# Two graph attention layers on one core: the second MLP product in 512 and 256 columns, with two sums added on VectorE, and new orders for all engines

## The chip, the core and the metric

One core of a Trainium2 chip runs the whole program. The metric is the device time of one execution in microseconds. Before the change it was 2083.72 us, the median of 3 runs (2083.6 to 2084.96).

## What is computed

x is 128 graphs x 128 nodes x 256 features in float32, adj a 128x128 matrix of 0 and 1 for each graph. Layer 0 is masked attention with 8 heads of 32, a residual and a normalisation. Layer 1 normalises, attends with a mask that also carries 0.1 x adj as a bias, adds the residual, normalises again and adds an MLP. Cut to what matters here:

```python
    x1 = residual + (out @ wo + bo)
    n2 = _ln(x1, ln2_g, ln2_b)
    mlp = jax.nn.gelu(n2 @ w1 + b1, approximate=False) @ w2 + b2      # w1 256x1024, w2 1024x256
    return x1 + mlp
```

## The kernel before, in words

**Tiling.** The 128 graphs are worked on in 32 groups b of G = 4 graphs; a group has T = 512 rows. A product whose operands carry real precision is split: each operand is a high part (float32r) and a low part, the remainder, and three products high x high, high x low and low x high are summed in PSUM (`split_mm`, lines 497 to 502, its matmuls at line 500). For q, k and the first MLP product (`qkv` n = 0 to 3, `mlp_up`) the moving operand has 512 columns; for v, the output projection and the second MLP product (`qkv` n = 4, 5, `out_proj`, `mlp_down`) it has 256.

**mlp_down(b, g)**, lines 557 to 567, takes graph g of a group: 8 chunks of 128 of the 1024 hidden features, three products each, the stationary operand being a chunk of h (high, high, low) and the moving one the 256 columns of w2 (high, low, high). Two graphs fill one PSUM bank ("MLP2", j), which VectorE adds to x1 in one operation of 128x512, `residual("MLP2", b, j)` (lines 972 to 981, the addition at 980).

**Attention.** `scores` (line 470) issues 32 small matmuls for half a group on 32-row tiles of the array. VectorE adds the mask and takes the maximum (`mask_scores`, 919), ScalarE takes the exponential (`exp`, 687), VectorE the reciprocal of the sum (`recip`, 935), GpSimd scales (`normalise`, 1147), TensorE transposes (`flip`, 482), ScalarE and VectorE copy the result into pt (`copy_pt`, 697 and 942), and `values` (493) multiplies by v, again in halves of 32 small matmuls. `flip_rows` (511) transposes the normalised rows for the next layer.

**Order.** Each engine has an order written out by hand: a head for groups 0 to 4, a body repeated for i = 5 to 30, which mixes stages of groups i + 1 to i - 3, and a tail. PSUM's 8 banks are handed out by the table JOBS (name, number, how many groups behind, bank); `open_job` makes TensorE wait until the bank's last user is done, `filled` makes a reader wait for TensorE, and `taken` waits for the reader. In the body before, the two halves of values of a group stand apart, with flips, products or transposes between them.

**Once, at the start.** The load of x for group 0 (transposed, xTr) is the first in ScalarE's DMA queue (line 660), ahead of the small table of columns (661). SyncE's queue starts with wq, wk, wv of layer 0 (384), then the two copies of adj. VectorE splits wq, wk and wv and then subtracts the high part of x (`x_lo`, 962). `second_products` (lines 445 to 456) makes 36 matmuls, 32 of them of one column at line 454, to fold constant shifts into biases; it needs w1 and stands behind the first out_proj of group 0's second half. `store` writes x1 out when the last MLP2 addition is done.

Of the kernel before, what the change touches and what calls it, by code (L numbers as in the profile page):

```python
# [160 lines left out]

def program(nc, x, xT, adj, w):
    ctx = ExitStack()
    with ctx:
# [1116 lines left out]
```

## Time and profile before

| what | us |
|---|---|
| median of 3 runs | 2083.72 |
| the profiled execution | 2083.27 |
| its span | 2081.5 |
| TensorE (PE) busy | 2039.3 |
| TensorE weight loads (PEld) busy | 1829.3 |
| ScalarE (ACT) busy | 1651.2 |
| VectorE (DVE) busy | 1596.7 |
| GpSimd (POOL) busy | 1008.5 |

The mean granted TensorE clock is 0.993 of full. Busy means that at least one instruction of the engine was in work. Matmuls overlap, so a record's duration (283 ns for 256 columns) is not what one adds: the distance from one start to the next is. The profiled execution's own time is 1.8 us more than its span, and 0.45 us less than the median.

### The profile page before, as it was taken

How to read it: one execution, taken by the hardware profiler on the slowest of the kernel's cores; microseconds unless marked ns; L12 is line 12 of the kernel's file. 1: busy time of each engine (PE TensorE's matmuls, PEld its weight loads, DVE VectorE, ACT ScalarE, POOL GpSimd, SP SyncE). 2: the span in 40 equal slices, each digit the busy share in tenths (PEclk: the TensorE clock that was granted, in tenths of full speed). 3: DMA queues.
4: the chain of work that ended last, by engine and by line, in shares of the span. 5: the costliest groups of instructions: out<-in, count | busy, mean ns of one | idle time of the engine just before them, and what ended most of it. 6: DMA issues, size and time to landing. Idle time of an engine off the chain costs nothing.

```text
span 2081.5 us, 58805 instructions
## 1 busy us (share of the span) xinstructions
PE 2039.3 (98%) x20032; PEld 1829.3 (88%) x20032; DVE 1596.7 (77%) x6915; ACT 1651.2 (79%) x5512; POOL 1008.5 (48%) x780
## 2 busy tenths in 40 slices
PE   6899999999999999999999999999999999999997
PEld 5688998889989889998889988889988899998886
DVE  6887877787877787777787777778777878777763
ACT  4788887888787878788888888887878887878873
POOL 3645445545445545445545445445455455455431
PEclk9999999999999999999999999999999999999999
DMA  5011110111110111100111100111101111101000
GB/s 155 17 32 42 43 38 15 30 41 41 40 34 14 33 40 41 41 19 21 40 41 41 40 10 30 41 40 41 38 13 30 41 41 40 35 15 31 27 12 21
DMA packets 80830, 73.18 MB, mean 35 GB/s; under 512 B 3024, under 2 KB 72272, under 8 KB 80720
## 3 DMA queue, kind: packets, MB, share of 16 engines
q1 hardware_dynamic: 80304, 71.45, 10.9%
q8 instruction: 36, 0.59, 0.1%
q14 instruction: 74, 0.61, 0.1%
q10 hardware_dynamic: 416, 0.54, 0.1%
HBM read 55.20 MB, written 16.78 MB: 35 GB/s over the span
## 4 chain that ended last, share of the span: by engine, by line
PE 96%; DVE 2%; ACT 1%; issue 0%; DMA 0%; POOL 0%; ACTq 0%; SPq 0%; DVEq 0%
PE ps L500 68%; PE ps L482 11%; PE ps L470 7%; PE ps L493 6%; PE ps L511 3%; ACT pm L687 1%; DVE pm L919 1%; DMA pm<-in_wk 0%; DVE stats L993 0%; PE ps L454 0%; DVE pt L942 0%; ACT k L721 0%; POOL pm L1147 0%; POOL rstd L1166 0%; DVE bv_rows L837 0%
## 5 line engine op out<-in xcount | busy, mean ns | idle before, releaser
L1147 POOL TENSOR_TENSOR pm<-pm,rinv 128x512 f32<-128x512 f32 x512 | 521.8, 1042 | 602.9 <-DVE rinv L935 602.7
L687 ACT ACTIVATE pm<-pm,nmax 128x128 f32<-128x128 f32 x2048 | 792.2, 392 | 10.1 <-DVE nmax L919 9.5
L919 DVE CUSTOM_DVE_ANT_0 pm<-ps,m 128x128 f32<-128x128 f32 x2048 | 456.4, 285 | 43.6 <-PE ps L470 42.5
L687 ACT ACTIVATION_READ_ACCUMULATOR pm<-pm,nmax 128x1 f32 x2048 | 392.3, 192 | 0.0
L500 PE MATMUL ps<-w2h,hh 128*128 128x256 f32 x1024 | 294.7, 288 | 2.2 <-DVE hl L1015 2.1
L482 PE MATMUL ps<-ident,pm 128*128 128x128 f32 x2048 | 289.7, 277 | 2.9 <-DVE v L968 1.8
L500 PE MATMUL ps<-w2h,hl 128*128 128x256 f32 x1024 | 289.6, 283 | 0.0
L500 PE MATMUL ps<-w2l,hh 128*128 128x256 f32 x1024 | 289.6, 283 | 0.0
L1166 POOL TENSOR_TENSOR rstd<-veps,power 128x4 f32<-128x4 f32 x96 | 97.3, 1014 | 362.4 <-DVE veps L1001 362.0
L482 PEld LDWEIGHTS ps<-ident,pm 128*128 128x128 f32 x2048 | 230.6, 140 | 45.6 <-issue 18.3
L942 DVE COPY pt<-ps 128x512 f32<-128x512 f32 x256 | 175.5, 687 | 104.7 <-PE ps L482 104.6
L697 ACT ACTIVATE pt<-ps 128x512 f32<-128x512 f32 x256 | 151.0, 591 | 105.8 <-PE ps L482 105.8
L1015 DVE TENSOR_TENSOR hl<-ps,hh 128x512 fp32r<-128x512 f32 x256 | 169.9, 681 | 61.5 <-ACT ps L745 58.0
L500 PE MATMUL ps<-acth,w1h 128*128 128x512 f32 x512 | 210.2, 410 | 3.8 <-DVE actl L956 3.8
L500 PE MATMUL ps<-acth,w1l 128*128 128x512 f32 x512 | 201.7, 394 | 0.0
L500 PE MATMUL ps<-actl,w1h 128*128 128x512 f32 x512 | 201.1, 393 | 0.0
L500 PEld LDWEIGHTS ps<-w2h,hh 128*128 128x128 f32 x1024 | 196.1, 192 | 4.2 <-DVE hl L1015 3.0
L500 PEld LDWEIGHTS ps<-w2l,hh 128*128 128x128 f32 x1024 | 196.3, 192 | 1.2
L500 PEld LDWEIGHTS ps<-w2h,hl 128*128 128x128 f32 x1024 | 196.1, 191 | 0.0
L744 ACT ACTIVATE hh<-ps,b 128x512 fp32r<-128x512 f32 x256 | 180.0, 703 | 14.1 <-PE ps L500 11.8
L745 ACT ACTIVATE ps<-ps,b 128x512 f32<-128x512 f32 x256 | 173.4, 677 | 0.0
L919 DVE DVE_READ_ACCUMULATOR2_ANT nmax<- 128x1 f32 x2048 | 170.2, 83 | 0.0
(123 smaller groups left out, 5058.7 us busy)
## 6 DMA issues: line engine op xcount, KB each, us to landing
xy<-in_x SPq DMA_DIRECT2D x32, 512.0 KB, 5.3
xTr<-in_xT SPq DMA_DIRECT2D x31, 512.0 KB, 4.5
out<-x SPq DMA_DIRECT2D x31, 512.0 KB, 3.0
m<-in_adj SPq DMA_DIRECT2D x32, 256.0 KB, 2.8
a<-in_adj SPq DMA_DIRECT2D x32, 256.0 KB, 2.8
pt<-in_w SPq DMA_DIRECT2D x2, 512.0 KB, 8.5
pt<-in_w SPq DMA_DIRECT2D x1, 1024.0 KB, 11.6
xTr<-in_xT ACTq DMA_DIRECT2D x1, 512.0 KB, 5.1
```

The lines of the kernel that those rows point to most:

```text
L470: last = mm(outs[r][:, at:at + N], q[l][rows, c, gs], k[l][rows, c, gs], start=True, stop=True)
L482: last = nc.tensor.transpose(out[:, j * N:(j + 1) * N], pm[:, g, c * HC + j, :], ident[:, :])
L493: last = mm(out[j * HD:(j + 1) * HD, at:at + N], v[l][:, g, h * HD:(h + 1) * HD], pt[:, pt_slot(l, g), place(h), :], start=True, stop=True)
L500: last = mm(out, pick(parts[a], c), wpick(wparts[b], c), start=(n == 0), stop=(n == len(terms) - 1))
L687: last = nc.scalar.activation(pm[:, g, h, :], pm[:, g, h, :], ACT.Exp, bias=nmax[:, g, h:h + 1], scale=-1.0, accum_out=rsum[:, g, h:h + 1])
L697: nc.scalar.activation(pt[:, pt_slot(l, g), 0:HC, :], src[:, :].rearrange("p (h q) -> p h q", h=HC), ACT.Copy).then_inc(free_of(f"F{l}", 2 ...
L744: nc.scalar.activation(hh[0][:, m, :], src[:, :], ACT.Gelu, bias=b1[:, m:m + 1])
L745: nc.scalar.activation(src[:, :], src[:, :], ACT.Gelu, bias=b1[:, m:m + 1]).then_inc(h_hi, 1)
L919: last = nc.vector.tensor_tensor_reduce(out=pm[:, g, h, :], in0=src[:, at:at + N], in1=m[:, g, :], scale=1.0, scalar=3e38, op0=ALU.add, op ...
L942: nc.vector.tensor_copy(pt[:, pt_slot(l, g), HC:H, :], src[:, :].rearrange("p (h q) -> p h q", h=HC))\
L1015: tt(hh[1][:, m, :], bank_of("MLP1", m)[:, :], hh[0][:, m, :].bitcast(F32), ALU.subtract).then_inc(free_of("MLP1", m), 1)
L1147: tt(pm[:, g, hs, :], pm[:, g, hs, :], rinv[:, g, hs].rearrange("p (h a) -> p h a", a=1).to_broadcast([P, HC, N]), ALU.mult).then_inc(norm ...
```

## The change

- mlp_down: for each chunk one product of 512 columns, the high part of h against both parts of w2, which now lie side by side in w2_both, and one of 256 columns, the low part of h against the high part of w2, summed into the right half of the bank. Each graph has a bank of its own. Two sums come out: left high x high, right the two cross terms.
- VectorE adds both to x1, one after the other, in operations of 128x256 (`residual_down`).
- The two halves of values of a layer stand next to each other in TensorE's order.
- The load of x for group 0 is second in SyncE's queue, behind wq. VectorE subtracts x's high part before it splits wk and wv, and wv is split only after mask0.
- second_products comes before the third flip of group 0.
- JOBS, HEAD, TAIL (the banks) and the orders of TensorE, ScalarE, VectorE and GpSimd are written anew.

```diff
-        w2 = [sb(f"w2{p}", [P, FC, D], F32R) for p in "hl"]
+        w2_both = sb("w2", [P, FC, 2, D], F32R)
+        w2 = [w2_both[:, :, p, :] for p in (0, 1)]
...
-                        taken(sp, b, "MLP2", j)
+                        taken(sp, b, "MLP2", 2 * j + 1)
...
-                    taken(sp, b, "MLP2", 1)
+                    taken(sp, b, "MLP2", G - 1)
...
+                    if n == 0:
+                        sp.dma_start(xTr[:, :, :], xT_v[:, :, 0:T]).then_inc(xT_loaded, 16)
...
+            def paired_mm(out, parts, pick, both, chunks):
+                for c in range(chunks):
+                    if c:
+                        mm(out[:, D:], pick(parts[1], c), both(c)[:, 0, :], start=False, stop=False)
+                    last = mm(out[:, :], pick(parts[0], c), both(c), start=(c == 0), stop=(c == chunks - 1))
+                    if c == 0:
+                        mm(out[:, D:], pick(parts[1], c), both(c)[:, 0, :], start=False, stop=False)
+                return last
...
-                    out = open_job(b, "MLP2", g // 2) if g % 2 == 0 else bank_of("MLP2", g // 2)
-                    last = split_mm(out[:, (g % 2) * D:(g % 2 + 1) * D], hh, w2,
-                                    lambda t, c: t[:, c, g * N:(g + 1) * N], lambda t, c: t[:, c, :], FC)
-                    if g % 2 == 1:
-                        full(last, "MLP2", g // 2)
+                    out = open_job(b, "MLP2", g)
+                    last = paired_mm(out, hh, lambda t, c: t[:, c, g * N:(g + 1) * N], lambda c: w2_both[:, c, :, :], FC)
+                    full(last, "MLP2", g)
...
-                sc.dma_start(xTr[:, :, :], xT_v[:, :, 0:T]).then_inc(xT_loaded, 16)
                 sc.dma_start(par[:, :], w["columns"]).then_inc(cols_loaded, 16)
...
+                        if l == 0 and first(b):
+                            dve.wait_ge(wqkv_lo[0], 3 * C)
...
+            def residual_down(b, g):
+                if exists(b):
+                    dve.wait_ge(x1b_done, b + 1)
+                    src = filled(dve, b, "MLP2", g)
+                    tt(x1[:, g, :], src[:, :D], x1[:, g, :], ALU.add).then_inc(half_sum, 1)
+                    dve.wait_ge(half_sum, slot(b, g) + 1)
+                    tt(x1[:, g, :], src[:, D:], x1[:, g, :], ALU.add).then_inc(free_of("MLP2", g), 1)
```

TensorE's body after, in full (that before is in the listing above):

```python
            def body(i):
                flip_rows("T2", i - 3, 1); scores(Y, i - 2, 0); flip(X, i - 1, 1, 1); flip(X, i - 1, 2, 0)
                mlp_up(i - 3, 0); mlp_up(i - 3, 1); flip(X, i - 1, 2, 1); mlp_up(i - 3, 2); flip(X, i - 1, 3, 0)
                mlp_up(i - 3, 3); flip(X, i - 1, 3, 1); mlp_up(i - 3, 4); values(X, i - 1, 0); values(X, i - 1, 1)
                mlp_up(i - 3, 5); mlp_up(i - 3, 6); mlp_up(i - 3, 7); out_proj(X, i - 1, 0); out_proj(X, i - 1, 1)
                scores(Y, i - 2, 1); flip(Y, i - 2, 0, 0); qkv(X, i, 0); qkv(X, i, 1); qkv(X, i, 2); qkv(X, i, 3)
                mlp_down(i - 3, 0); mlp_down(i - 3, 1); flip(Y, i - 2, 0, 1); scores(X, i, 0); flip(Y, i - 2, 1, 0)
                flip(Y, i - 2, 1, 1); mlp_down(i - 3, 2); mlp_down(i - 3, 3); flip(Y, i - 2, 2, 0); qkv(X, i, 4)
                flip(Y, i - 2, 2, 1); flip(Y, i - 2, 3, 0); flip(Y, i - 2, 3, 1); qkv(X, i, 5)
                flip_rows("T1", i - 1, 0); values(Y, i - 2, 0); values(Y, i - 2, 1); scores(X, i, 1)
                flip_rows("T1", i - 1, 1); flip(X, i, 0, 0); out_proj(Y, i - 2, 0); out_proj(Y, i - 2, 1)
                flip(X, i, 0, 1); flip(X, i, 1, 0); qkv(Y, i - 1, 0); qkv(Y, i - 1, 1); qkv(Y, i - 1, 2)
                qkv(Y, i - 1, 3); qkv(Y, i - 1, 4); qkv(Y, i - 1, 5); flip_rows("T2", i - 2, 0)
```

The part of VectorE's body around the new additions:

```python
                residual("WO0", i - 1, 1); mask_scores(Y, i - 2, 2, 0); mask_scores(Y, i - 2, 2, 1)
                mask_scores(Y, i - 2, 3, 0); mask0(i); recip(Y, i - 2, 1); norm_stats(0, i - 1)
                mask_scores(Y, i - 2, 3, 1); norm_rows(0, i - 1); residual_down(i - 3, 0); residual_down(i - 3, 1)
                recip(Y, i - 2, 2); copy_pt(Y, i - 2, 0); mask_scores(X, i, 0, 0); mask_scores(X, i, 0, 1)
                recip(Y, i - 2, 3); flipped(Y, i - 2, 1, 0); mask_scores(X, i, 1, 0); flipped(Y, i - 2, 1, 1)
                mask_scores(X, i, 1, 1); residual_down(i - 3, 2); norm_stats(1, i - 1); copy_pt(Y, i - 2, 1)
                residual_down(i - 3, 3); norm_rows(1, i - 1); copy_pt(Y, i - 2, 2); copy_pt(Y, i - 2, 3)
```

The new JOBS gives MLP2's four products the banks 6, 4, 6 and 7; flip (1, 1) of layer 1 has bank 4, and the scores of X, half 0, have banks 7, 0, 3 and 1.

## Rows read from the trace of the kernel before

**Rows 1.** The page: busy us and count of two engines; the chain by engine.
```profile
PE 2039.3 (98%) x20032; PEld 1829.3 (88%) x20032; DVE 1596.7 (77%) x6915; ACT 1651.2 (79%) x5512; POOL 1008.5 (48%) x780
...
PE 96%; DVE 2%; ACT 1%; issue 0%; DMA 0%; POOL 0%; ACTq 0%; SPq 0%; DVEq 0%
```

**Rows 2.** TensorE's waits: who waited for whom, us in total, times, longest.
```profile
PE ps L493 <- DVE pt L942: 3.8, 1, 3.8
```

**Rows 3.** Busy us (and count) of PE, PEld, DVE, ACT, POOL by stretch; clock; DMA.
```profile
968.60:1031.60 63.00, 63.00 (x625) 56.63 (x625) 49.24 (x215) 51.39 (x173) 31.27 (x25) 1.00 0.11 34
...
276.00:1913.00 1637.00, 1637.00 (x16224) 1471.95 (x16223) 1279.93 (x5591) 1335.50 (x4473) 812.35 (x625) 1.00 0.11 34
```

**Rows 4.** TensorE's timeline, 1028 to 1040 us: start, duration, instruction.
```profile
1029.10 0.39 PE L500 MATMUL ps<-actl,wqkv0h 128*128 128x512 f32 x1
...
1032.98 0.28 PE L500 MATMUL ps<-w2h,hh 128*128 128x256 f32 x1
1033.09 0.28 PE L500 MATMUL ps<-w2l,hh 128*128 128x256 f32 x1
...
1038.73 0.40 PE L500 MATMUL ps<-acth,wqkv0h 128*128 128x512 f32 x1
...
1039.20 0.39 PE L500 MATMUL ps<-acth,wqkv0l 128*128 128x512 f32 x1
```

**Rows 5.** Weight loads by line and form: busy us, mean ns, idle before.
```profile
L500 PEld LDWEIGHTS ps<-w2h,hl 128*128 128x128 f32 x1024 | 196.1, 191 | 0.0
```

**Rows 6.** TensorE's timeline, 1043 to 1047 us.
```profile
1043.96 1.17 PE L470 MATMUL ps<-k,q 32*128 32x128 f32 x32
...
1046.07 1.09 PE L482 MATMUL ps<-ident,pm 128*128 128x128 f32 x8
1046.92 0.36 PE L500 MATMUL ps<-w2h,hh 128*128 128x256 f32 x1
```

**Rows 7.** The weight loads' timeline in the same stretch.
```profile
1045.06 0.81 PEld L493 LDWEIGHTS ps<-pt,v 128*32 128x32 f32 x32
1046.07 0.86 PEld L482 LDWEIGHTS ps<-ident,pm 128*128 128x128 f32 x8 [0.20 <-issue]
```

**Rows 8.** VectorE by line and form: busy us, mean ns, idle before.
```profile
L980 DVE TENSOR_TENSOR x<-ps,x 128x512 f32<-128x512 f32 x64 | 42.6, 665 | 12.9 <-PE ps L500 12.9
...
L998 DVE BATCH_NORM_AGGREGATE mv<-stats 128x2 f32<-128x6 f32 x384 | 36.8, 157 | 14.4 <-issue 0.4
...
L873 DVE TENSOR_TENSOR bo<-bo,ps 128x256 f32<-128x256 f32 x1 | 0.4, 408 | 0.0
```

**Rows 9.** The timeline of all engines, 0 to 12 us.
```profile
0.74 0.51 ACTq L660 DMA_DIRECT2D xTr<-in_xT  x1
...
6.73 0.49 DVE L825 TENSOR_SCALAR wqkv0h<-pm 128x256 fp32r<-128x256 f32 x2
6.92 0.20 ACT L656 ACTIVATE nbq<-par 128x2 f32<-128x2 f32 x1 [3.85 <-DMA par<-in_columns]
7.16 1.15 ACT L737 ACTIVATE acth<-xTr 128x512 fp32r<-128x512 f32 x2
...
9.60 1.29 DVE L962 TENSOR_TENSOR actl<-xTr,acth 128x512 fp32r<-128x512 f32 x2
...
11.04 0.77 PE L500 MATMUL ps<-acth,wqkv0h 128*128 128x512 f32 x1 [11.04 <-DVE actl L962]
```

**Rows 10.** The chain that ended last, in order of time.
```profile
45.96 4.43 PE ps L454 x32
```

**Rows 11.** DMA issues: KB each, median us from issue to landing.
```profile
pt<-in_w SPq DMA_DIRECT2D x2, 512.0 KB, 8.5
...
xTr<-in_xT ACTq DMA_DIRECT2D x1, 512.0 KB, 5.1
```

**Rows 12.** The timeline of all engines, 2078 us to the end.
```profile
2077.83 0.28 PE L500 MATMUL ps<-w2h,hl 128*128 128x256 f32 x1
2078.21 0.69 DVE L980 TENSOR_TENSOR x<-ps,x 128x512 f32<-128x512 f32 x1 [5.07 <-PE ps L500]
```

More of the change, by code:

```diff
@@ L642, in tail @@
                 mlp_down(30, 1); mlp_down(30, 2); flip(Y, 31, 1, 0); flip(Y, 31, 1, 1); mlp_down(30, 3)
-                flip(Y, 31, 2, 0); flip(Y, 31, 2, 1); flip(Y, 31, 3, 0); flip(Y, 31, 3, 1); values(Y, 31, 0)
-                values(Y, 31, 1); out_proj(Y, 31, 0); out_proj(Y, 31, 1); flip_rows("T2", 31, 0)
+                flip(Y, 31, 2, 0); flip(Y, 31, 2, 1); flip(Y, 31, 3, 0); flip(Y, 31, 3, 1)
+                values(Y, 31, 0); values(Y, 31, 1); out_proj(Y, 31, 0); out_proj(Y, 31, 1); flip_rows("T2", 31, 0)
@@ L847, in split_q, with split_kv, first_rows @@
                 split_part(0, -SCALE)
[L849 removed]
+            def split_kv(b, n):
                 if first(b):
[L851 to L852 removed]
+                    split_part(n, 1.0)
+            def first_rows(b):
+                if first(b):
                     dve.wait_ge(cols_loaded, 16)
@@ L1060, in head @@
-                split_h(1, 4); out_lo(X, 3, 1); split_h(1, 5); mask0(4); split_h(1, 6); x_lo(4, 0); x_lo(4, 1)
-                residual("WO0", 3, 1); split_h(1, 7); norm_stats(0, 3); mask_scores(Y, 2, 2, 0); recip(Y, 2, 1)
-                norm_rows(0, 3); mask_scores(Y, 2, 2, 1); copy_pt(Y, 2, 0); mask_scores(Y, 2, 3, 0)
-                residual("MLP2", 1, 0); copy_pt(Y, 2, 1); recip(Y, 2, 2); mask_scores(Y, 2, 3, 1); norm_stats(1, 3)
-                recip(Y, 2, 3); mask_scores(X, 4, 0, 0); mask_scores(X, 4, 0, 1); mask_scores(X, 4, 1, 0)
@@ L1065, in head @@
-                mask_scores(X, 4, 1, 1); out_lo(Y, 2, 0); norm_rows(1, 3); v_out(X, 4, 0); recip(X, 4, 0)
-                residual("MLP2", 1, 1); v_out(X, 4, 1); copy_pt(Y, 2, 2); copy_pt(Y, 2, 3); lo("T1", 3, 0)
-                lo("T1", 3, 1); mask1(3); out_lo(Y, 2, 1); mask_scores(X, 4, 2, 0); residual("WO1", 2, 0)
-                mask_scores(X, 4, 2, 1); recip(X, 4, 1); residual("WO1", 2, 1); mask_scores(X, 4, 3, 0)
-                norm_stats(2, 2); mask_scores(X, 4, 3, 1); copy_pt(X, 4, 0); norm_rows(2, 2); v_out(Y, 3, 0)
@@ new lines, in head @@
+                copy_pt(X, 0, 1); copy_pt(X, 0, 2); split_qkv1(0, 1); copy_pt(X, 0, 3); out_lo(X, 0, 0); x_lo(1, 0)
+                x_lo(1, 1); out_lo(X, 0, 1); residual("WO0", 0, 0); mask0(1); residual("WO0", 0, 1); norm_stats(0, 0)
+                norm_rows(0, 0); mask_scores(X, 1, 0, 0); mask_scores(X, 1, 0, 1); mask_scores(X, 1, 1, 0)
+                mask_scores(X, 1, 1, 1); norm_stats(1, 0); v_out(X, 1, 0); v_out(X, 1, 1); recip(X, 1, 0)
+                norm_rows(1, 0); mask_scores(X, 1, 2, 0); lo("T1", 0, 0); lo("T1", 0, 1); recip(X, 1, 1)
@@ new lines, in head @@
+                mask_scores(X, 1, 2, 1); mask_scores(X, 1, 3, 0); copy_pt(X, 1, 0); split_w1(0, 0); recip(X, 1, 2)
+                mask_scores(X, 1, 3, 1); split_w1(0, 1); v_out(Y, 0, 0); mask_scores(Y, 0, 0, 0); recip(X, 1, 3)
+                mask_scores(Y, 0, 0, 1); mask_scores(Y, 0, 1, 0); flipped(X, 1, 1, 1); mask_scores(Y, 0, 1, 1)
+                copy_pt(X, 1, 1); copy_pt(X, 1, 2); copy_pt(X, 1, 3); v_out(Y, 0, 1); out_lo(X, 1, 0); recip(Y, 0, 0)
+                x_lo(2, 0); mask0(2); residual("WO0", 1, 0); recip(Y, 0, 1); x_lo(2, 1); mask_scores(Y, 0, 2, 0)
@@ new lines, in head @@
+                out_lo(Y, 0, 0); lo("T1", 1, 0); out_lo(Y, 0, 1); mask_scores(X, 2, 2, 0); mask_scores(X, 2, 2, 1)
+                lo("T1", 1, 1); recip(X, 2, 1); residual("WO1", 0, 0); residual("WO1", 0, 1); mask_scores(X, 2, 3, 0)
+                norm_stats(2, 0); copy_pt(X, 2, 0); mask_scores(X, 2, 3, 1); norm_rows(2, 0); mask1(1); recip(X, 2, 2)
+                v_out(Y, 1, 0); lo("T2", 0, 0); lo("T2", 0, 1); mask_scores(Y, 1, 0, 0); mask_scores(Y, 1, 0, 1)
+                mask_scores(Y, 1, 1, 0); copy_pt(X, 2, 1); mask0(3); recip(X, 2, 3); copy_pt(X, 2, 2); v_out(Y, 1, 1)
@@ new lines, in head @@
+                flipped(X, 2, 1, 1); mask_scores(Y, 1, 1, 1); copy_pt(X, 2, 3); split_h(0, 0); split_h(0, 1)
+                out_lo(X, 2, 0); split_h(0, 2); split_h(0, 3); split_h(0, 4); split_h(0, 5); out_lo(X, 2, 1)
+                x_lo(3, 0); x_lo(3, 1); residual("WO0", 2, 0); recip(Y, 1, 0); split_h(0, 6); residual("WO0", 2, 1)
+                split_h(0, 7); norm_stats(0, 2); mask_scores(Y, 1, 2, 0); mask_scores(Y, 1, 2, 1); recip(Y, 1, 1)
+                mask_scores(Y, 1, 3, 0); mask_scores(Y, 1, 3, 1); norm_rows(0, 2); residual_down(0, 0)
@@ new lines, in head @@
+                lo("T1", 2, 1); mask_scores(X, 3, 2, 1); residual("WO1", 1, 0); residual("WO1", 1, 1); recip(X, 3, 1)
+                mask_scores(X, 3, 3, 0); norm_stats(2, 1); mask_scores(X, 3, 3, 1); copy_pt(X, 3, 0); norm_rows(2, 1)
+                mask1(2); recip(X, 3, 2); v_out(Y, 2, 0); lo("T2", 1, 0); lo("T2", 1, 1); mask_scores(Y, 2, 0, 0)
+                mask_scores(Y, 2, 0, 1); recip(X, 3, 3); mask_scores(Y, 2, 1, 0); copy_pt(X, 3, 1)
+                flipped(X, 3, 1, 1); mask_scores(Y, 2, 1, 1); recip(Y, 2, 0); copy_pt(X, 3, 2); copy_pt(X, 3, 3)
@@ new lines, in head @@
+                split_h(1, 0); v_out(Y, 2, 1); split_h(1, 1); out_lo(X, 3, 0); split_h(1, 2); out_lo(X, 3, 1)
+                split_h(1, 3); mask0(4); split_h(1, 4); split_h(1, 5); x_lo(4, 0); residual("WO0", 3, 0)
+                split_h(1, 6); x_lo(4, 1); split_h(1, 7); residual("WO0", 3, 1); mask_scores(Y, 2, 2, 0)
+                norm_stats(0, 3); mask_scores(Y, 2, 2, 1); mask_scores(Y, 2, 3, 0); mask_scores(Y, 2, 3, 1)
+                recip(Y, 2, 1); norm_rows(0, 3); residual_down(1, 0); copy_pt(Y, 2, 0); residual_down(1, 1)
@@ new lines, in head @@
+                residual("WO1", 2, 0); residual("WO1", 2, 1); mask_scores(X, 4, 3, 0); norm_stats(2, 2)
+                mask_scores(X, 4, 3, 1); copy_pt(X, 4, 0); norm_rows(2, 2); mask1(3); recip(X, 4, 2); v_out(Y, 3, 0)
+                lo("T2", 2, 0); lo("T2", 2, 1); mask_scores(Y, 3, 0, 0); recip(X, 4, 3); mask_scores(Y, 3, 0, 1)
+                mask_scores(Y, 3, 1, 0); flipped(X, 4, 1, 1); mask_scores(Y, 3, 1, 1); copy_pt(X, 4, 1)
+                copy_pt(X, 4, 2); recip(Y, 3, 0); v_out(Y, 3, 1); copy_pt(X, 4, 3); split_h(2, 0); split_h(2, 1)
```

484 lines of the change are left out of this document (221 added, 263 removed), and 137 rows, old and new, of tables (HEAD, JOBS, TAIL).

## The prediction, made before the changed kernel ran

> **What bounds the kernel now.** I began with the page's busy times and chain [rows 1]: TensorE is busy for 2039.3 of 2081.5 us and 96% of the chain that ended last is its matmuls; VectorE has a quarter of the span free. As a busy share proves little for pipelined matmuls, I next asked for TensorE's waits [rows 2]. They are few, and all of them lie in the first 110 us or the last 110: the same question for 276 to 1913 us returned no line. The table of stretches [rows 3] says so in another way: in one loop of 62.97 us (968.6 to 1031.6, repeated 26 times) TensorE has no idle time, VectorE is busy for 49.24 us, ScalarE for 51.39 and the clock is granted in full. So in the loop only a shorter stream of TensorE instructions saves time, and work put on another engine is free until it makes TensorE wait.
>
> The profiled execution took 2083.27 us, 1.8 beyond its span; the median of the runs is 2083.72, 0.45 more. I work from 2083.27. About 0.2% (4 us) is what a measurement of this kernel can tell from no change.
>
> **The paired product.** For each of 8 chunks of h and 4 batch rows, mlp_down issued three products of 256 columns; now there is one of 512 (high h against both parts of w2) and one of 256 (low h): 1024 chunks in 32 groups, 2048 matmuls in place of 3072, over the same 768 columns. The timeline [rows 4] gives the pace from start to start: 48 matmuls of 256 columns take 5.75 us (1032.98 to 1038.73), 119.8 ns each; 17 of 512 columns take 3.88 us (1029.10 to 1032.98), 228 ns each. Two of 256 cost 240 ns, one of 512 costs 228. A chunk goes from 359.4 to 228 + 119.8 = 348 ns: 11.4 ns x 1024 = **11.7 us saved**. No row shows the two lengths alternating, as they will now, so I bound a pair by the changeovers: the first two of 512 after a run of 256 took 0.47 us, 235 ns each (pair 355 ns, 4.5 us saved), and the first of 256 after one of 512 took 0.11 (pair near 339, 21 us saved). I take the middle, since it is what each has in its own run, and keep both ends.
>
> Every matmul comes with a weight load of its own, which lasts 192 ns in the records [rows 5] and yet is issued every 119.8, so loads overlap matmuls here. The Trainium skill ("TensorE: Matmul & The Clock Gate", Back-to-back issue gap) gives 262 cycles for 256 columns and 518 for 512, so by it three become one and one for 6 cycles, an estimated 2.5 ns a chunk and 2.6 us in all, which speaks against most of this gain. What the rows would make of such a rule is the first rival below.
>
> **A layer's values as one step.** values ran as two halves of 32 small matmuls with other work between; now both halves of a layer stand together. One half takes 1.01 us (1045.06 to 1046.07) and scores 1.10 [rows 6, 7]. The weight path stood idle for 0.20 us behind the half before it could turn to flips [rows 7]. Inside a half one group of 4 follows another every 0.09 to 0.11 us (32 in 0.81 us of loads), so a half that follows a half should save 0.20 - 0.09 = 0.11 us. In the loop the counts are equal otherwise: scores and values form five runs per loop before and five after, and two borders between scores and values become two between halves. 62 pairs x 0.11 = **6.8 us saved** (nothing if the border stays, 12 if all 0.20 goes).
>
> **The other order of TensorE.** By the two written orders, the loop has 13 runs of flips and transposes in place of 12. Their own work is the same; 8 flips behind values took 0.85 us (1046.07 to 1046.92) [rows 6], and a run of them between products adds to its neighbours some 0.02 us by such differences: 32 x 0.02 = 0.6 us lost, taken between 0 and 2.
>
> **VectorE.** Two residual additions of 128x512 at 665 ns a loop (1.33 us) become eight of 128x256. The one of that size that also reads PSUM took 408 ns [rows 8]: 3.26 us, and four of them wait for the one before. A wait of that kind, the aggregation behind its statistics, cost 14.4 us in 96 times, 0.15 each: 0.6 us. In all 2.5 us a loop onto 49.24 of 62.97. It is taken at nothing, covered by VectorE's 13.7 us of idle time; where that cover isn't in the right place is the second rival. MLP2 also uses four PSUM banks a group instead of two (6, 4, 6, 7), each free after its second addition; and the store of the output waits for the last one, and the addition of WO1 for the store, with some 9 us of VectorE work between. ScalarE and GpSimd do the same work in another order: nothing. The strided w2 is written once, before its use: nothing.
>
> **The start.** The load of x goes from ScalarE's queue at 0.74 us to second in SP's, some 0.5 later; the columns are then first in ScalarE's queue, and wk, wv, the masks and all later loads of SP go 0.5 us later. ScalarE waited for the columns until 6.92, copied x from 7.16 [rows 9], and had both halves by 8.31, but VectorE subtracted x only at 9.60, behind the splits of wk and wv, which began at 6.73. TensorE began at 11.04. In the new order the subtraction stands ahead of them: its second half can start at 8.4 and end at 9.1, TensorE starts near 9.2, and the split of wk ends some 1.3 us later (both took 2.5), well before the products of k, which stand behind 12 matmuls of q. x landing 0.5 later still meets ScalarE's 7.16 (it landed at 5.84, 5.1 behind its issue) [rows 11]. **1.7 us saved** of a possible 1.9; nothing if a later load is what the chain then meets.
>
> second_products moves from behind the first out_proj to before the flips of group 0. Its 32 small matmuls were 4.43 us of the chain [rows 10]; TensorE waited 3.8 us for pt close behind where they now stand [rows 2]. They could be hidden whole, but w1, which they read, is a load of 8.5 us late in SP's queue [rows 11] and the chain then meets other waits, so I take **1.5 us saved** (0 to 4.4).
>
> **The end.** After the last matmul one addition of 0.69 us led to the last store [rows 12]. Now it is two dependent ones, 0.41 + 0.15 + 0.41: **0.3 us lost**.
>
> The sum: -11.7 - 6.8 + 0.6 - 1.7 - 1.5 + 0.3 = -20.8, so 2083.3 - 20.8 = **2062.5 us**.
>
> **Rivals.** *A, the two columns' worth is all there is (0.17).* A 512 product behind a 256 product always costs what the first two did, 235 ns, and the pair 355: 4.5 us instead of 11.7, so 2069.7 us. For it: each 512 now stands behind a 256. Against: in the same rows the 512 is slow for only a few matmuls, and the 256 after it is fast. By the skill's own cycle counts it would be 2.6 instead of 11.7, which lies beside this.
>
> *B, the pair is faster than its parts (0.15).* If 119.8 is the pace of the weight load and the 256 columns alone need half of 228, then a 512 before it leaves time for the load and the pair takes about 341: 18.8 us saved, 2055.4 us. For it: the 0.11 us after a 512 [rows 4]. Against: the load for the 512 must still fit under a 256.
>
> *C, small waits in the loop (0.14).* The waits gained are smaller than the savings: 0.3 us a loop, 26 times, gives 2062.5 + 8 = 2070.5 us. For it: a fresh order of every engine. Against: the old order, made in the same way, had no wait in 26 loops.
>
> *D, VectorE becomes the bound (slower; 0.07).* Its place: the flip (1,1) of Y goes to bank 4, that of mlp_down's second product. From the end of that product to this flip TensorE has one flip, scores and one flip, about 0.4 + 1.1 + 0.5 = 2.0 us, in which VectorE must see it (0.4, the distance at the end of the kernel [rows 12]) and do both additions (1.0). It decides from the point at which VectorE comes to residual_down over 0.6 us late; behind it are the mask additions of the next scores, whose banks the last mlp_down needs. To lose, TensorE must wait over (20.8 + 4.2) / 26 = 0.96 us a loop. At 1.2 us a loop the time is 2062.5 + 31 = 2093.7. Against: VectorE's chain from the preceding scores (masks 3 x 0.85, mask0 0.4, statistics 2.6, a root and rows 2.7) ends near 8.7 us, while the first product of mlp_down ends at about the same time and the second 2.8 later.
>
> *E, the gains stay and the values save nothing (0.05)*: 2069.3 us. That the change isn't what it says has no room: the widths and counts follow from the code.
>
> **The numbers.** The forecast has 0.42. It, A, B, C and E are all faster by over 4 us, 0.93; some of C could be larger waits that eat most of the gain, so I move 0.04 to no change and 0.01 to slower: 0.88 faster, 0.04 the same, 0.08 slower. The range reaches from B with a better head (2055.4 - 2.9 = about 2052) to A or C with the values' 6.8 lost (2076.5, taken as 2076); D and the rest of B lie outside.
>
> **What would show it.** Right: the loop, read as the distance of one line's repeats, is 62.4 us (62.97 less 0.36 and 0.22) without a TensorE wait; in mlp_down a 512 and a 256 together advance by 348 ns; a half of values behind a half takes 0.9 us; TensorE's first matmul starts at 9.2 us; the first product follows x's subtraction; the additions take 0.41 us each. Wrong: a wait of TensorE for the MLP2 additions, for masks or for pt inside the loop; a pair at 355 or 341; a first matmul still near 11 us; head waits that grew by what the start gained.

## The result and the profile after

The changed kernel takes **2076.35 us** (median of 6 runs, 2073.25 to 2078.65), beside 2084.34 for the kernel before: ratio 0.9961, 95% interval 0.995 to 0.9971. That is 8 us faster, 0.35 us outside the forecast range and 14 us short of the forecast gain of 20.8. The profiled execution took 2076.95 us with a span of 2075.2 (before 2083.27 and 2081.5).

The page of the changed kernel, busy times and chain, against [rows 1]:

```profile
PE 2028.0 (98%) x19008; PEld 1782.2 (86%) x19008; DVE 1655.5 (80%) x7107; ACT 1654.2 (80%) x5512; POOL 1005.0 (48%) x780
PE 96%; DVE 3%; issue 1%; DMA 1%; ACT 0%; SPq 0%; POOL 0%; ACTq 0%; DVEq 0%
```

**The loop did what was forecast.** TensorE's timeline in it, of the products of mlp_down and of values:

```profile
972.58 0.28 PE L518 MATMUL ps<-w,hl 128*128 128x256 f32 x1
972.70 0.40 PE L519 MATMUL ps<-w,hh 128*128 128x512 f32 x1
972.93 0.28 PE L518 MATMUL ps<-w,hl 128*128 128x256 f32 x1
973.05 0.40 PE L519 MATMUL ps<-w,hh 128*128 128x512 f32 x1
...
974.70 0.28 PE L518 MATMUL ps<-w,hl 128*128 128x256 f32 x1
...
928.74 1.95 PE L502 MATMUL ps<-pt,v 128*32 128x128 f32 x64
...
991.13 1.95 PE L502 MATMUL ps<-pt,v 128*32 128x128 f32 x64
```

A 256 and a 512 advance by 0.35 us together (the six pairs from 972.58 to 974.70 take 2.12, 353 ns each; three of the loop's four mlp_down steps give 347 to 352 a pair, the one that begins behind flips 363), and the same step, the first half of Y's values, repeats after 991.13 - 928.74 = 62.39 us against 62.97 [rows 3]. 0.58 us in 26 passes are 15.1. TensorE waits for nothing between 276 and 1913 us, as before [rows 2]. VectorE's two additions, where [rows 8] had one of 128x512 (busy us, mean ns of one, idle before):

```profile
L998 DVE TENSOR_TENSOR x<-ps,x 128x256 f32<-128x256 f32 x128 | 54.3, 424 | 4.4
L996 DVE TENSOR_TENSOR x<-ps,x 128x256 f32<-128x256 f32 x128 | 53.9, 421 | 73.5 <-PE ps L519 68.7
```

At the end, the last matmul, the two additions and the store follow as forecast, 0.2 us later behind TensorE's end than before.

**The start gained more.** The timeline of the first microseconds, against [rows 9]:

```profile
3.65 0.49 DVE L841 TENSOR_SCALAR wqkv0h<-pm 128x256 fp32r<-128x256 f32 x2 [3.65 <-DMA pm<-in_wq]
5.59 1.15 ACT L753 ACTIVATE acth<-xTr 128x512 fp32r<-128x512 f32 x2 [2.76 <-DMA xTr<-in_xT]
6.25 1.29 DVE L982 TENSOR_TENSOR actl<-xTr,acth 128x512 fp32r<-128x512 f32 x2 [1.31 <-ACT acth L753]
7.69 0.77 PE L509 MATMUL ps<-acth,wqkv0h 128*128 128x512 f32 x1 [7.69 <-DVE actl L982]
```

TensorE starts at 7.69 us, 3.3 sooner than before and 1.5 sooner than forecast.

**The head and the tail gave it back.** Stretches of the kernel before, then of the changed one, each from TensorE's first matmul. Columns: stretch, its length, then busy us and count of TensorE, its weight loads, VectorE, ScalarE and GpSimd, the granted clock, DMA share and GB/s.

```profile
11.00:150.00 139.00, 123.26 (x1196) 106.59 (x1197) 108.27 (x474) 100.57 (x355) 71.90 (x54) 0.95 0.18 55
1913.00:2078.20 165.20, 153.08 (x1366) 137.29 (x1364) 101.92 (x406) 109.19 (x338) 60.66 (x47) 0.96 0.05 17
```

```profile
7.70:150.00 142.30, 120.47 (x1117) 104.40 (x1118) 111.11 (x465) 95.56 (x346) 67.54 (x50) 0.90 0.19 62
150.00:276.00 126.00, 126.00 (x1191) 110.58 (x1189) 104.28 (x444) 104.05 (x347) 66.66 (x51) 1.00 0.11 35
1913.00:2071.60 158.60, 144.50 (x1200) 123.92 (x1198) 103.20 (x389) 99.78 (x303) 56.85 (x44) 0.96 0.05 18
```

In the head TensorE is idle for 142.3 - 120.5 = 21.8 us, before for 15.7. Its granted clock is at half (1.2 GHz in place of 2.4) for 27.3 us (the records' stretches 21.6 to 28.4, 35.2 to 38.6, 55.7 to 59.1, 66.0 to 72.8, 93.3 to 96.7 and 106.9 to 110.3), before for 13.7; it is busy in these for 24.5 and 13.0 us, and work at half clock takes twice its time, so that is 12.3 and 6.5 us. Idle time and clock together are 34.1 against 22.2 us: **the head gave back 11.9 us**. In the tail the clock takes the same as before and small waits add 2.0 us (idle 14.1 against 12.1). The whole of it: start -3.3, TensorE's work at full speed without waits -17.1 (15.1 of it in the loop), head +11.9, tail +2.0, end +0.2, together -6.3, which is what the span shows.

Where the new head waits, by TensorE's waits from 7 to 150 us (engine, tile, line, released by; us in total, times, longest):

```profile
PE ps L531 <- DVE xy L1036: 6.0, 2, 4.5
PE ps L509 <- DVE nmax L939: 4.9, 2, 3.0
PE ps L509 <- issue: 2.2, 2, 1.9
PE ps L479 <- issue: 2.1, 1, 2.1
```

The second longest (3.0 us) is at bank 0, which the new JOBS gives both to qkv(X,1,4) and to a score (before, that product had bank 7, which none of the scores of half 0 has). The longest, 4.5 us, is TensorE waiting at 61 us for VectorE's normalised rows of group 0, which it then flips as T1. VectorE's and GpSimd's timelines there:

```profile
60.56 0.19 DVE L955 RECIPROCAL rinv<-rsum 128x8 f32<-128x8 f32 x1
60.67 4.80 DVE L1036 TENSOR_SCALAR xy<-y,mv,rstd 128x256 f32<-128x256 f32 x4
...
60.83 2.14 POOL L1180 TENSOR_TENSOR pm<-pm,rinv 128x512 f32<-128x512 f32 x2 [1.27 <-DVE rinv L955]
62.94 2.38 POOL L1208 TENSOR_TENSOR r<-y,bo 128x1024 f32<-128x1024 f32 x1
```

Four row instructions take 4.80 us, where one takes 0.41 elsewhere. The reciprocal ahead of them had just released GpSimd; the first one is done at 61.03, and the other three end at 62.08, 63.12 and 65.47 us, 0.15 us behind the ends of GpSimd's three, 61.93, 62.97 and 65.32.

In the kernel before, VectorE's order had the rows ahead of that reciprocal, and they took 1.38 us; TensorE's wait for them was there too, but shorter. VectorE's timeline, then the wait:

```profile
63.87 1.38 DVE L1008 TENSOR_SCALAR xy<-y,mv,rstd 128x256 f32<-128x256 f32 x4
65.16 0.20 DVE L935 RECIPROCAL rinv<-rsum 128x8 f32<-128x8 f32 x1
```

```profile
PE ps L511 <- DVE xy L1008: 3.3, 1, 3.3
```

### The profile page after: what moved, and what is told of

It reads as the page before. It is cut to its first block, busy times and chain, and to the rows that moved or that the text cites. A ratio compares the mean times of both kernels' runs of the same rounds, so it can differ in the third digit from the quotient of the medians.

```text
span 2075.2 us, 57260 instructions
## 1 busy us (share of the span) xinstructions
PE 2028.0 (98%) x19008; PEld 1782.2 (86%) x19008; DVE 1655.5 (80%) x7107; ACT 1654.2 (80%) x5512; POOL 1005.0 (48%) x780
## 4 chain that ended last, share of the span: by engine, by line
PE 96%; DVE 3%; issue 1%; DMA 1%; ACT 0%; SPq 0%; POOL 0%; ACTq 0%; DVEq 0%
PE ps L509 52%; PE ps L519 11%; PE ps L491 11%; PE ps L479 7%; PE ps L502 6%; PE ps L518 5%; PE ps L531 3%; PE ps L521 1%; DVE pm L939 1%; DVE xy L1036 0%; DMA m<-in_adj 0%; DMA xTr<-in_xT 0%; DVE stats L1021 0%; PE ps L463 0%; DVE actl L982 0%
## 5 line engine op out<-in xcount | busy, mean ns | idle before, releaser
L519 PE MATMUL ps<-w,hh 128*128 128x512 f32 x1024 | 363.4, 399 | 2.5 <-DVE hl L1043 2.4
L491 PEld LDWEIGHTS ps<-ident,pm 128*128 128x128 f32 x2048 | 236.7, 142 | 32.9 <-issue 3.4
L518 PE MATMUL ps<-w,hl 128*128 128x256 f32 x896 | 249.9, 279 | 0.0
L962 DVE COPY pt<-ps 128x512 f32<-128x512 f32 x256 | 169.2, 679 | 66.4 <-PE ps L491 66.2
L519 PEld LDWEIGHTS ps<-w,hh 128*128 128x128 f32 x1024 | 188.0, 188 | 39.1 <-DVE hl L1043 3.1
L1043 DVE TENSOR_TENSOR hl<-ps,hh 128x512 fp32r<-128x512 f32 x256 | 172.0, 682 | 60.9 <-ACT ps L761 60.6
L509 PE MATMUL ps<-acth,w1h 128*128 128x512 f32 x512 | 215.3, 421 | 5.0 <-DVE actl L976 3.9
L518 PEld LDWEIGHTS ps<-w,hl 128*128 128x128 f32 x896 | 168.9, 189 | 5.7
L479 PE MATMUL ps<-k,q 32*128 32x128 f32 x4096 | 151.1, 284 | 5.1 <-ACT k L737 2.2
L479 PEld LDWEIGHTS ps<-k,q 32*128 32x128 f32 x4096 | 126.8, 187 | 27.6 <-issue 22.3
```

Source lines behind the costliest of these rows:

```text
L479: last = mm(outs[r][:, at:at + N], q[l][rows, c, gs], k[l][rows, c, gs], start=True, stop=True)
L491: last = nc.tensor.transpose(out[:, j * N:(j + 1) * N], pm[:, g, c * HC + j, :], ident[:, :])
L509: last = mm(out, pick(parts[a], c), wpick(wparts[b], c), start=(n == 0), stop=(n == len(terms) - 1))
L518: mm(out[:, D:], pick(parts[1], c), both(c)[:, 0, :], start=False, stop=False)
L519: last = mm(out[:, :], pick(parts[0], c), both(c), start=(c == 0), stop=(c == chunks - 1))
L962: nc.vector.tensor_copy(pt[:, pt_slot(l, g), HC:H, :], src[:, :].rearrange("p (h q) -> p h q", h=HC))\
```

## The experiments

Each was timed against the kernel before, in runs on the same chip; ratios are to it. Differences are between medians, in us. Kernels e1 to e4, e6, e7, e9 and e10 are edits of the changed kernel (2076.35). Not all were timed on one chip; beside them the kernel before had medians of 2084.11 to 2084.60, so a difference of 0.5 us between two of them says nothing. The diffs are shortened.

**e1: the paired product undone.**

```diff
-mm(out[:, D:], low_h, w2_high); mm(out[:, :], high_h, both)
+mm(out[:, D:], low_h, w2_high)
+mm(out[:, :D], high_h, w2_high); mm(out[:, D:], high_h, w2_low)   # in 7 of 8 chunks
```

> The changed kernel, but with the paired product undone in 7 of 8 chunks: high h meets the high and the low part of w2 in two products of 256 columns, low h in a third, as before the change (the first chunk stays a pair, since it opens the bank). Order of work, banks, sums and additions stay. Theory (the loop gains what was forecast, the head gives it back): a chunk is again 359 to 360 ns in place of the 347 to 350 that the changed kernel's trace shows, so 10 to 12 ns x 7 x 128 = 9 to 11 us more, 2085.5 to 2087.5 us, with 62.7 us for a pass of the loop. Rival (the pair is worth less than half of its term and the rest of the loop's gain is the order's): at most 5 us more, under 2081.5 us.

2084.70 us (+8.4), ratio 1.0005 (0.9996 to 1.0014). TensorE's timeline, the same step in two successive passes:

```profile
934.77 1.95 PE L502 MATMUL ps<-pt,v 128*32 128x128 f32 x64
...
997.44 1.96 PE L502 MATMUL ps<-pt,v 128*32 128x128 f32 x64
```

A pass takes 62.67 us, 0.28 more for 28 chunks: 10.0 ns a chunk, 10.2 us for 1024. The time is a little under the 2085.5 to 2087.5 expected and well above the rival's 2081.5. The forecast had 11.4 and 11.7. The paired product is right; without it the change would gain nothing.

**e2: the halves of values apart, in the loop.**

```diff
-values(X, i - 1, 0); values(X, i - 1, 1); mlp_up(i - 3, 5)
+values(X, i - 1, 0); mlp_up(i - 3, 5); values(X, i - 1, 1)
-flip_rows("T1", i - 1, 0); values(Y, i - 2, 0); values(Y, i - 2, 1)
+values(Y, i - 2, 0); flip_rows("T1", i - 1, 0); values(Y, i - 2, 1)
```

> The changed kernel, but inside the loop (26 passes) the two halves of values stand apart again: an mlp_up between those of X, the flips of T1's first half between those of Y. Theory: two halves in a row take 1.88 us in the changed trace against 2 x 1.01 apart, 0.14 us a pair; 52 pairs are 7.3 us more, 2083.6 us, a pass of 62.66 us. Rival (what the second half saves, its other neighbours lose, so that being adjacent is worth nothing): 0 to 2 us more, a pass of 62.39 to 62.46 us.

2091.53 us (+15.2), ratio 1.0036 (1.0023 to 1.005).

```profile
932.36 1.08 PE L502 MATMUL ps<-pt,v 128*32 128x128 f32 x32
933.95 1.08 PE L502 MATMUL ps<-pt,v 128*32 128x128 f32 x32
...
995.37 1.08 PE L502 MATMUL ps<-pt,v 128*32 128x128 f32 x32
```

The pass is 63.01 us, 0.62 more, over twice the theory's 0.27 and far from the rival's 0 to 0.07. By the starts of each step, the halves themselves give 0.28 (1.01 each in place of 0.90 and 0.99); the rest falls on what now stands beside a border: 0.23 on the mlp_up behind a half, 0.09 on a v product ahead of one, 0.05 on the flips between two. So a border costs the neighbours of values as well, and a second one costs again.

**e3: x first, in ScalarE's queue.**

```diff
 SP:      -load xT(0) behind wq
 ScalarE: +load xT(0) ahead of the columns
```

> The changed kernel, but x is loaded by ScalarE's queue first, as before the change; the subtraction of x's low part stays ahead of the splits of wk and wv. Theory one (the start passes into the time): wq lands at 5.3 and x at 6.9 us as before the change, TensorE starts near 9.2 in place of 7.69 us, and the time is 1.5 us more, 2077.9 us. Theory two (the head waits for VectorE and ScalarE a little later anyway, so that an earlier start is lost there): the same start near 9.2, and the time within 0.5 us of 2076.4 us.

2077.72 us (+1.4), ratio 0.9966 (0.9955 to 0.9978), an interval that holds the changed kernel's 0.9961, so the two theories aren't told apart. TensorE started at 8.70 us against 7.69: of the 3.3 us of earlier start, 1.0 comes from the queue and 2.3 are there without it. Not all of the 2.3 is the order of VectorE's steps: the columns released ScalarE at 6.37 us where the kernel before, with the same first loads, had 6.92. That 0.55 us is a difference between two profiled executions, and leaves some 1.8 for the order.

**e8: the new start in the kernel before.**

```diff
 SP:      +load xT(0) behind wq        ScalarE: -load xT(0)
-split_kv(0); x_lo(0, 0); x_lo(0, 1)
+x_lo(0, 0); x_lo(0, 1); split_kv(0)
```

> The kernel before, with the start of the changed one alone: x second in the queue of the loads, and x's low part ahead of the splits of wk and wv. Theory one (an earlier start passes into the time where the head's order is otherwise as before): TensorE starts at 7.7 us in place of 11.0, and 2 to 3.3 us are gained, 2081 to 2082 us. Theory two (the head's middle is bound by VectorE's masks and by ScalarE's exp, and the start is lost in their waits): under 1 us gained, above 2083.2 us.

2081.20 us, 3.4 less than the kernel before; ratio 0.9985 (0.9976 to 0.9994). TensorE starts at 8.01, 3.0 sooner. By the medians the old head lets an earlier start through whole; the interval allows 1.3 to 5.0 us.

**e4: the rows ahead of the reciprocal.**

```diff
-recip(X, 1, 0); norm_rows(1, 0)
+norm_rows(1, 0); recip(X, 1, 0)
-recip(X, 2, 0); norm_rows(1, 1)
+norm_rows(1, 1); recip(X, 2, 0)
```

> The changed kernel, with two pairs of VectorE's steps in the head swapped: the normalised rows of layer 1 for groups 0 and 1 come before the reciprocal behind which they stood. That reciprocal lets GpSimd start to normalise scores, and in the changed trace each of the four row instructions at 60.67 to 65.47 us then ends with a GpSimd instruction: 4.80 us where four take 1.4. Theory (GpSimd beside them stretches them, and TensorE's wait of 4.5 us for T1 comes of it): they take 1.4 us, TensorE's wait there falls to about 1.3 us, the clock falls less often, and the time is 3 to 5 us less, 2071.5 to 2073.5 us. Rival (the wait only moves to what stands behind it, the reciprocal and the scores): less than 1 us gained, above 2075.4 us.

2068.85 us (-7.5), ratio 0.9928 (0.9914 to 0.9941), where 3 to 5 us less was expected. VectorE and GpSimd in the same stretch:

```profile
60.66 1.37 DVE L1036 TENSOR_SCALAR xy<-y,mv,rstd 128x256 f32<-128x256 f32 x4
61.95 0.20 DVE L955 RECIPROCAL rinv<-rsum 128x8 f32<-128x8 f32 x1
...
62.22 2.04 POOL L1179 TENSOR_TENSOR pm<-pm,rinv 128x512 f32<-128x512 f32 x2 [3.44 <-DVE rinv L955]
```

The rows take 1.37 us, TensorE waits 0.9 in place of 4.5, and its head has 17.2 us of idle time and 12.5 busy at half clock: 23.5 us, 10.6 less. (Its profiled execution is 9.3 us below that of the changed kernel; by the medians it is 7.5.)

**e9: GpSimd's addition of a bias row moved, VectorE untouched.**

```diff
-add_bo1(0); normalise(X, 1, 1, 0); normalise(X, 1, 1, 1)
+normalise(X, 1, 1, 0); normalise(X, 1, 1, 1); add_bo1(0)
```

> The changed kernel, with one step of GpSimd alone moved: the addition of the bias row of layer 1 for group 0 (2.38 us, 62.94 to 65.32 in the changed trace) comes two normalisations later. VectorE's order stays, so the reciprocal is still ahead of the rows. Theory (VectorE's row instructions wait for whatever GpSimd runs): the fourth of them ends near 63.4 in place of 65.47 us, TensorE's 4.5 us wait shrinks to about 2.5, and 2 to 4 us are gained with the clock, 2072.5 to 2074.5 us. Rival (it was the place of the reciprocal that counted in e4_rows_ahead, not what GpSimd ran beside the rows): no gain, 2075.9 us or more.

2071.71 us (-4.6), ratio 0.9947 (0.9934 to 0.9961).

```profile
60.95 0.19 DVE L955 RECIPROCAL rinv<-rsum 128x8 f32<-128x8 f32 x1
61.06 2.78 DVE L1036 TENSOR_SCALAR xy<-y,mv,rstd 128x256 f32<-128x256 f32 x4
...
61.22 2.14 POOL L1180 TENSOR_TENSOR pm<-pm,rinv 128x512 f32<-128x512 f32 x2 [2.14 <-DVE rinv L955]
```

With one of GpSimd's three instructions gone from beside them, the fourth row instruction takes 0.40 us in place of 2.42, and all four 2.78. TensorE's wait is 2.3 us in place of 4.5. The reciprocal is still ahead, so it isn't its place that counts but what GpSimd runs. How much time that is worth stays rough: the five runs lie at 2071.21 to 2075.28, the interval overlaps that of the changed kernel, and by means the gain is 3.1 us. The stretching did not vanish either: the moved addition now makes VectorE's split of w1 at 69.4 us last 2.86 us (0.74 in the changed kernel), where TensorE doesn't wait for it.

**e10: the first of the two swaps alone.**

> The changed kernel with the first of the two swaps of e4_rows_ahead alone: the rows of T1 of group 0 ahead of the reciprocal of group 1. Theory (the 4.5 us wait at 61 us and the clock that falls behind it carry most of the 7.5 us that both swaps gained): 2069.5 to 2071 us. Rival (the gain is spread over both): 2072 to 2073 us.

2072.20 us (-4.2), ratio 0.9938 (0.9924 to 0.9951), runs 2068.48 to 2073.85. This is in the rival's range: by the medians the second swap, for group 1 at 114 us, carries 3.3 of the 7.5 us; the two intervals overlap, so the shares are rough.

**e5: the head mended.** e4 and three more moved steps:

```diff
 VectorE: -residual("WO0", 0, 0); mask0(1); residual("WO0", 0, 1); norm_stats(0, 0)
          +residual("WO0", 0, 0); residual("WO0", 0, 1); norm_stats(0, 0); mask0(1)
          -shifts(0) with rows_of(1, 1) at its end; v_out(X, 0, 0)
          +shifts(0) with v_out(X, 0, 0) ahead of rows_of(1, 1)
 GpSimd:  -lo_w2(0, 1) behind normalise(Y, 0, 0, 1)
          +lo_w2(0, 1) behind lo_w2(0, 0)
```

> As e4_rows_ahead (2068.85 us), with three more steps moved in the head, all after what its trace and that of the changed kernel show: GpSimd takes the second half of w2's low part right behind the first (its 2.4 us stretched x's subtraction at 90.05 to 2.69 us and the mask at 87.73); VectorE makes mask0 of group 1 behind the statistics of group 0, where it waits for GpSimd anyway, not ahead of the residual (2.12 us beside GpSimd where 0.44 is usual); VectorE copies v of group 0 ahead of the rows of bv, which took 1.68 us beside GpSimd and held the bank for TensorE's 2.6 us wait. Theory (each of these stretched steps is on the path): 1.4 + 0.7 + about 2 us less, 2064 to 2066 us. Rival (TensorE waits next for the banks of the scores, whose masking sets the head): within 1 us of 2068.85 us.

**2063.41 us** (-12.9; 4 runs, 2062.92 to 2064.25), ratio 0.99 (0.9885 to 0.9915). It beats both kernels, and is a little better than the 2064 to 2066 expected. That it lies 0.9 us from the forecast for the changed kernel is luck: the terms of that sum came out otherwise, as the next section shows. Idle time is 14.9 us and busy time at half clock 11.0: 20.4 us, less than the head of the kernel before.

**e11: e5 with second_products late**, in the 3.0 us wait behind scores(X,1,0) and in bank 5; VectorE's additions of their result, second_shifts(0), move along.

```diff
-qkv(X, 0, 5); second_products(0); flip(X, 0, 1, 0)
+qkv(X, 0, 5); flip(X, 0, 1, 0)
-scores(X, 1, 0); qkv(X, 1, 4)
+scores(X, 1, 0); second_products(0); qkv(X, 1, 4)
```

> As e5_head_mended (2063.41 us), but the products of the second layer's bias rows (36 products, some 4.4 us) stand in TensorE's 3.0 us wait behind the first scores of group 1, in another bank, in place of their new place between v and the flips of group 0. This undoes the early place to which the prediction gave 1.5 us. Theory one (the early place fills a wait for pt that comes back without it, as the 3.8 us of the kernel before): 3 to 4 us come back at 30 us, 3 are filled at 52, and the time is within 1.5 us of 2063.41 us. Theory two (in the new head that wait no longer exists, and the 3.0 us are filled for nothing): 2 to 4 us less, 2059.5 to 2061.5 us.

2067.93 us, 4.5 more than e5; ratio 0.9923 (0.9909 to 0.9937). This is neither theory's number. One line of its waits of TensorE says why:

```profile
PE ps L491 <- POOL pm L1178: 4.3, 5, 2.0
```

Without the products there, TensorE waits 4.3 us for GpSimd's normalised scores of group 0. In their late place they fill the 3.0 us, but take 4.7 (54.30 to 58.98), and T1 starts at 66.1 us in place of 61.9.

**e7: one of the two additions left out** (`tt(x1, src[:, :D], x1)`: high h by high w2 isn't in the result).

> The changed kernel without the first of the two additions of each batch row (the left 256 columns, high h by high w2, are left out of the result): 128 VectorE instructions of about 0.4 us fewer, 1.6 us in a pass. Theory (TensorE bounds the loop, VectorE's additions are covered): the pass stays 62.39 us, and the time is 0.4 us less from the very last addition, up to 1.5 us less if the head's masks come sooner. Rival (the additions hold up banks or masks): 5 us or more less, a shorter pass.

2075.75 us (-0.6), ratio 0.9961 (0.9946 to 0.9977), a pass of 62.39 us to the hundredth. The additions cost the loop nothing.

**e6 and e12: a wait filled with work that nothing reads**, to keep the clock up: e6 in the changed kernel ahead of T1, e12 in e5 behind scores(X,1,0).

```diff
+for _ in range(18):   # e12: 12, in a bank free until group 1's flips
+    mm(out[:, :], wqkv[0][0][:, 0, 0:P], wqkv[0][0][:, 0, 0:T], start=True, stop=True)
```

> The changed kernel, with 18 products of 512 columns that nothing reads put into TensorE's 4.5 us wait for the rows of T1 of group 0 (4.1 us at the full clock), into the bank that the flips then overwrite. Everything waits as before; only the clock can change. Theory (of the 12 us that the head gave back, half is TensorE's work at the 0.5 clock after waits: 24.5 us of busy time at half clock against 13.0 before the change): the half-clock stretch of 66.0 to 72.8 us behind that wait goes or shrinks, 1.5 to 3.4 us less, 2073 to 2075 us. Rival (the clock falls whatever stands in that wait, or VectorE sets the pace there): 2076.4 us, or up to 1 us more where the filling runs past the wait.

> As e5_head_mended (2063.41 us), with 12 products of 512 columns that nothing reads in TensorE's 3.0 us wait behind the first scores of group 1 (2.7 us at the full clock), into a bank that is free until group 1's flips. In e5's trace the clock is at half from 52.7 to 59.5 us, right behind that wait. Theory (a head's wait costs a second time, by the half clock behind it: some 2.7 to 3.4 us for that stretch): the half-clock stretch goes and 2 to 3.4 us are gained, 2060 to 2061.5 us. Rival (TensorE's work in that stretch is hidden by VectorE's chain of masks, statistics and rows, so that the clock costs nothing there): the stretch goes from the trace and the time stays, 2062.5 to 2064.5 us.

e6: 2075.92 us (-0.4; 2073.60 to 2079.00), ratio 0.9962 (0.9948 to 0.9975). e12: 2063.54 us (+0.1 on e5; 2062.57 to 2065.52), ratio 0.9899 (0.9883 to 0.9916). Both follow the rival in time by their medians, and neither quite in the reason. In e6 the profiled execution was one of its two shortest (2074.20 and 2073.60): there the stretch behind the wait is gone, TensorE is busy at half clock for 17.7 us of the head in place of 24.5, and the first mlp_down comes 3.0 us sooner. But two of the changed kernel's own six runs are as short (2073.25, 2073.84), so this doesn't show a gain. The windows of e5, then of e12, columns as above:

```profile
50.00:60.00 10.00, 6.73 (x64) 6.44 (x68) 6.21 (x43) 6.44 (x33) 5.49 (x3) 0.66 0.01 2
90.00:101.00 11.00, 8.62 (x81) 7.40 (x80) 9.34 (x58) 10.52 (x44) 9.28 (x7) 1.00 0.01 1
```

```profile
50.00:60.00 10.00, 8.44 (x100) 7.13 (x100) 7.78 (x47) 6.52 (x33) 5.62 (x3) 1.00 0.01 2
90.00:101.00 11.00, 8.63 (x75) 7.70 (x74) 9.29 (x60) 9.43 (x38) 8.23 (x6) 0.84 0.01 1
```

The clock stays at full in 50 to 60 us, and T1's flips start at 60.24 in place of 61.87. But then it is at half from 97.5 to 100.9, behind a wait of 1.9 us at which e5 kept it, and by the values at 103.2 us the 1.6 us are gone (103.3 in e5). Filling a wait took away the half-clock stretch behind it, and a fall behind a later wait took the gain back.

**e13: e5 with v_out(X,1,1) behind the rows.**

> As e5_head_mended (2063.41 us), with VectorE's copy of the second half of v of group 1 behind the rows of T1 instead of ahead of them. Theory (VectorE's chain through rows and T1 sets the head there): GpSimd's root is done at 59.6 us and the rows start at once in place of 1.0 us later, 1 us less, or 2 with the clock, 2061.4 to 2062.4 us. Rival (TensorE at half clock sets the pace there): no gain, 2063 us or more.

2063.20 us (-0.2 on e5), ratio 0.99 (0.9883 to 0.9916). T1 starts at 60.6 us in place of 61.9, and at the first mlp_down 0.6 us of that are left. The times don't tell theory and rival apart at this size.

## Why the prediction was wrong

Right, point by point: the paired product (10.0 ns a chunk by e1, 347 to 352 ns a pair and 363 in one step of four; forecast 11.4 and 348); the loop (62.39 us, forecast 62.4), without a wait; VectorE's additions at nothing (e7), 0.42 us each where 408 ns were taken; the end (0.2 us, forecast 0.3). Rivals A, B, C and D are refuted by these rows, and E by e2. The Trainium skill's rule ("TensorE: Matmul & The Clock Gate", Back-to-back issue gap) would have given an estimated 2.5 ns a chunk where e1 shows 10.

The term for **values** came out in sum and not in its working. A half behind a half saves 0.14 us (0.11 was taken), and e2 shows that parting the halves costs 0.31 us a pair in this order, 0.17 of it at the neighbours. Two pairs are 0.62 us a pass; but of the loop's 0.58 the paired product has 0.32, which leaves 0.26 for everything that moved. So the forecast 62.4 us was right in sum by luck: other borders of the new order cost back what the term left out, and which ones was not tried.

The term for **the start** was half its size: 3.3 us in the trace and 3.4 in e8, where 1.7 of "a possible 1.9" stood. I had kept the landing of wq at its old time. But x no longer shares the first microseconds with it: wq was there at 3.65 us in place of 5.31 (3.54 in e8, where x also stands second in SyncE's queue, and 4.93 in e3, where it goes first in ScalarE's), and ScalarE, which no longer waited for the columns behind x, copied x at 5.59 in place of 7.16.

**second_products** was taken at 1.5 us of 0 to 4.4. e11 shows 4.5 us between its new place and one still later than the old; what the move from the old place gave was not measured.

**The step that failed** is the sentence "ScalarE and GpSimd do the same work in another order: nothing", and beside it VectorE's own new order, which had no term at all: only its additions in the loop were costed. The range followed from that: no case let the head lose more than the start gains, and "head waits that grew" stood only among the signs. (Its upper end was worked out at 2076.5 and then taken as 2076, so 2076.35 lies within 0.2 us of a case, A with the values' gain lost, that did not happen; nothing is to be read from so near a miss.) The head lost 11.9 us. e4 and e10 by their times, and e9 by its trace, show the largest single cause: row instructions of VectorE last until a running GpSimd instruction has ended, and the new order set the reciprocal that starts GpSimd ahead of rows that TensorE waits for; before, it stood behind them. An estimate from the traces says the same for the whole head: VectorE's instructions that last over 0.15 us longer than the median of their kind do so by 4.5 us in all in the kernel before, 11.4 in the changed one, 6.5 in e4 and 4.5 in e5. In e9 the sum stays at 11.3, so what matters is whether TensorE waits for the stretched one. The first look at the head should have asked, for each of VectorE's steps that TensorE waits for, what the new order puts on GpSimd beside it. The Trainium skill has the rule, and I had not weighed it ("SBUF — State Buffer", SBUF: two separate sides): the port pair that the two engines share is held by one of them for a whole instruction, and the other waits; on VectorE's side this holds for an instruction in a two-port mode or with two inputs in SBUF. The trace agrees, with 0.15 us between GpSimd's end and VectorE's.

Of the rest, e5's three other moves carry 5.4 us together and weren't tried singly. Two waits of the new head remain in e5: the 3.0 us for the bank that qkv(X,1,4) shares with a score, which by the two JOBS tables goes back to the reassigned banks, and 1.9 us of the same kind in group 2. No run gave these products other banks, so what the new JOBS cost stays open.

**How much is the clock.** Runs of one kernel differ in it by themselves: the changed kernel's six stand at mean clocks of 0.990 (2076.95, 2077.24, 2078.65 us), 0.991 (2075.75) and 0.992 (2073.84, 2073.25). Over the 81 runs of the 14 kernels other than the one before, each against its own kernel's mean, 0.001 of mean clock goes with 1.2 us (correlation -0.76). 0.001 of the clock over 2075 us is 2.1 us of full-speed work, so some 0.6 of what the clock takes is seen in the time. The two profiled executions, 0.993 and 0.990, differ by an estimated 3.7 us from this, less than the 5.8 that the half-clock stretches of the two traces give. That a wait behind slow work is shorter would explain it, but no run tests it. So a third to a half of the 12 us is the clock, and the rest is waits. How much exactly stays open: this is a correlation, and the two experiments that filled a wait didn't move the median.

The tail's 2.0 us weren't tried. By the waits there they are many small ones (0.7 us the largest new one, a flip behind a mask).

## What to carry to other kernels

When a change is made by giving every engine a new written order, cost the loop by its stream of matmuls and the head on its own: there each order is run once, nothing is behind to cover it, and a wait can be paid a second time in the clock. Before one engine's steps are called hidden, look at what else they hold up: here two reciprocals, each one place too early, put GpSimd beside VectorE's rows and cost 7.5 us, almost what the whole change gained. The remedy is cheap, since it is a matter of order: let the step that releases GpSimd come behind the VectorE step, all in SBUF, that the critical engine waits for.
